# Two graph layers over 64 graphs on one core: the orders of all five engines and the PSUM banks replaced by a new plan

## The reference, cut to what matters

```
# layer 0                                    (adj holds 0 or 1 here)
q, k  = x@Wq+bq, x@Wk+bk
attn  = softmax(q k^T / sqrt(32))            # unmasked, per head
out   = sum_r (attn * (adj==r)) @ (x@Wv[r]+bv[r])
x1    = LN(x + out@Wo + bo) * g1 + beta1
x2    = LN(x1 + gelu(x1@W1+b1)@W2 + b2) * g2 + beta2
# layer 1
e     = leaky_relu(q k^T, 0.2) from x2@Wq, x2@Wk
h     = softmax(where(adj>0, e, -9e15)) @ (x2@Wv)
n1    = LN(h) * g1 + b1
out   = LN(concat(n1, x2) @ Wffn^T) * g2 + b2 + x2
```

## Time and profile before

| | before |
|---|---|
| median of 3 runs | 3199.16 us |
| the runs | 3191.37, 3199.16, 3201.94 us |
| span of the profiled execution | 3190.8 us |
| instructions in the profile | 76499 |
| busy: PE, PEld, DVE, ACT, POOL | 97%, 85%, 82%, 64%, 45% |
| granted TensorE clock, mean | 0.989 |

### The profile page before, as it was taken

One profiled execution on the slowest core, in us unless ns is written; L12 is line 12 of the kernel. 1 busy time (PEld: TensorE's weight loads), 2 busy tenths in 40 slices (PEclk: granted clock), 3 DMA queues, 4 the chain that ended last, 5 costly groups with the idle time before them and its releaser, 6 DMA issues.

```text
span 3190.8 us, 76499 instructions
## 1 busy us (share of the span) xinstructions
PE 3103.2 (97%) x28139; PEld 2715.8 (85%) x28328; DVE 2604.6 (82%) x4896; ACT 2056.7 (64%) x4303; POOL 1432.6 (45%) x1549
## 2 busy tenths in 40 slices
PE   5999999999999999999999999999999999999996
PEld 4888888888888888888888888888888888888885
DVE  4788888888888888888888888888888888888884
ACT  2565766766766766766766766766766766666664
POOL 1445445445445445445445445445344444444441
PEclk8999999999999999999999999999999999999997
DMA  4343344344334334434434434433433433433431
GB/s 111 84 101 93 89 94 97 89 92 98 91 89 98 94 86 98 96 83 98 99 81 98 102 79 97 105 79 94 107 79 92 110 79 89 112 80 89 107 81 31
DMA packets 218074, 292.76 MB, mean 92 GB/s; under 512 B 31796, under 2 KB 119479, under 8 KB 218039
## 3 DMA queue, kind: packets, MB, share of 16 engines
q1 hardware_dynamic: 218038, 292.30, 39.0%
HBM read 73.02 MB, written 16.78 MB: 28 GB/s over the span
## 4 chain that ended last, share of the span: by engine, by line
PE 90%; ACT 3%; issue 3%; DVE 2%; SPq 1%; DMA 1%; POOL 0%; POOLq 0%; DVEq 0%; ACTq 0%
PE pair L994 50%; PE pair L1024 15%; PE pair L1048 7%; PE pair L1038 6%; PE pair L1103 4%; PE pair L1112 2%; PE pair L1040 2%; ACT probs L561 2%; PE pair L1012 2%; SPq L299 1%; PE pair L999 1%; PE pair L1119 0%; ACT leaky_s L540 0%; DMA stack_a<-qk 0%; DMA probs<-in_w 0%
## 5 line engine op out<-in xcount | busy, mean ns | idle before, releaser
L418 POOL TENSOR_TENSOR act_r_lo<-act,act_r_hi 128x512 fp32r<-128x512 f32 x256 | 335.3, 1319 | 741.6 <-DVE act_r_hi L931 537.5
L540 ACT ACTIVATE leaky_s<-leaky_s,low_r 128x256 f32<-128x256 f32 x1024 | 506.1, 499 | 2.7 <-DVE low_r L794 2.0
L424 POOL TENSOR_TENSOR probs<-probs,rel 128x512 f32<-128x512 f32 x256 | 293.4, 1168 | 207.0 <-ACT probs L561 119.8
L561 ACT ACTIVATE probs<-pair 128x1024 f32<-128x1024 f32 x256 | 256.8, 1029 | 189.9 <-PE pair L1112 189.9
L798 DVE TENSOR_REDUCE mx_a<-pair 128x4 f32<-128x1024 f32 x256 | 307.7, 1223 | 78.1 <-PE pair L1103 78.0
L534 ACT ACTIVATE leaky_s<-pair 128x1024 f32<-128x1024 f32 x256 | 262.6, 1026 | 158.7 <-PE pair L1040 158.7
L790 DVE TENSOR_TENSOR leaky_s<-pair,leaky_s 128x1024 f32<-128x1024 f32 x256 | 312.4, 1220 | 37.8 <-ACT leaky_s L534 37.5
L794 DVE TENSOR_REDUCE low_r<-leaky_s 128x4 f32<-128x1024 f32 x256 | 310.8, 1214 | 2.2
L530 ACT ACTIVATE probs<-pair 128x1024 f32<-128x1024 f32 x256 | 261.8, 1023 | 65.1 <-PE pair L1048 60.9
L424 POOL TENSOR_TENSOR leaky_s<-probs,rel 128x512 f32<-128x512 f32 x256 | 291.0, 1173 | 0.2 <-ACT probs L561 0.2
L1048 PE MATMUL pair<-ident,leaky_s 128*128 128x128 f32 x2048 | 269.7, 275 | 6.7 <-ACT leaky_s L540 5.8
(11 more groups left out here) (193 smaller groups left out, 8839.7 us busy)
## 6 DMA issues: line engine op xcount, KB each, us to landing
stack_a<-qk SPq DMA_DIRECT2D x768, 128.0 KB, 2.5
stack_r<-qk SPq DMA_DIRECT2D x768, 128.0 KB, 2.4
xt<-in_xT SPq DMA_DIRECT2D x64, 256.0 KB, 3.4
adj_a<-in_adjT SPq DMA_DIRECT2D x64, 256.0 KB, 3.0
xn<-in_x SPq DMA_DIRECT2D x64, 256.0 KB, 3.2
adj_q<-in_adj SPq DMA_DIRECT2D x64, 256.0 KB, 2.9
out<-n SPq DMA_DIRECT2D x64, 256.0 KB, 2.8
probs<-in_w SPq DMA_DIRECT2D x4, 512.0 KB, 4.6
```

The costliest lines, as they stand in the source:

```text
L418: return nc.gpsimd.tensor_tensor(dst, src, hi, ALU.subtract)
L424: last = nc.gpsimd.tensor_tensor(masked_p[g][:, h], probs[:, g, h], rel1[:], ALU.mult)
L540: last = nc.scalar.activation(leaky_s[:, p % SLOTS, k, t], leaky_s[:, p % SLOTS, k, t], ACT.Exp, bias=low_r[:, p, k, t:t + 1], accum_out=d ...
L561: return nc.scalar.activation(probs[:, g, 2 * q:2 * q + 2], pair[b][:], ACT.Exp, scale=SCALE)
```

## The change

```diff
-        B_AO, B_ADEN, B_Q, B_K, B_WO, B_X1T, B_RV, B_HN = 2, 6, 7, 6, 1, 4, 4, 2
-        B_DN, B_N1T, B_FFN, B_AMT, B_X2T, B_LQ, B_LK, B_LV = 1, 1, 3, 4, 1, 4, 7, 7
+        B_AO, B_ADEN, B_Q, B_K, B_WO, B_X1T, B_RV, B_HN = 3, 2, 2, 4, 1, 5, 7, 5
+        B_N1T, B_DN, B_FFN, B_AMT, B_X2T, B_LQ, B_LK, B_LV = 6, 0, 1, 1, 0, 7, 5, 4
         B_X = 0
-        B_V, B_UP = (5, 7), (4, 6, 1, 5)
-        B_RR, B_TN, B_AR, B_AC = (0, 2, 1, 0), (0, 1, 1, 3), (3, 1, 2, 3), (2, 3, 2, 0)
+        B_V, B_UP = (0, 1), (4, 5, 3, 4)
+        B_RR, B_TN, B_AR, B_AC = (3, 2, 1, 0), (3, 3, 3, 1), (3, 1, 3, 2), (3, 1, 3, 2)
 
         ld_xt, ld_xn, ld_adj_a = sig("ld_xt", 16), sig("ld_xn", 16), sig("ld_adj_a", 16)
...
 def body(g0, g1, g2, g3):
-    if g2 is not None:
-        load(xn, x, g2, "(t p) c -> p t c", ld_xn)
...
+        if ran(g2, 1):
+            sp.wait_ge(off_done.sem, off_done.at(g2 - 1))
+        load(adj_q, adj, g2, "(t p) n -> p t n", ld_adj_r)
     if g1 is not None:
         sp.wait_ge(rqk_split.sem, rqk_split.at(g1))
         stack(0, stack_r, stacked_r)
         stack(1, stack_r, stacked_r)
         stack(2, stack_r, stacked_r)
         stack(3, stack_r, stacked_r)
-    if g2 is not None:
-        load(adj_q, adj, g2, "(t p) n -> p t n", ld_adj_r)
-    if g3 is not None:
+    if g3 is not None:
+        if ran(g3, 1):
+            sp.wait_ge(res_a_done.sem, res_a_done.at(g3 - 1))
+        load(xn, x, g3, "(t p) c -> p t c", ld_xn)
         sp.wait_ge(qk_split.sem, qk_split.at(g3))
         stack(0, stack_a, stacked_a)
         stack(1, stack_a, stacked_a)
         stack(2, stack_a, stacked_a)
         stack(3, stack_a, stacked_a)
-        load(adj_a, adjT, g3, "(t p) n -> p t n", ld_adj_a)
     if g0 is not None:
         sp.wait_ge(ln_done[LN_O].sem, ln_done[LN_O].at(g0))
         sp.dma_start(out[g0 - path.general * G].rearrange("(t p) c -> p t c", p=P), result[:]).then_inc(stored.sem, 16)
+    if g3 is not None:
+        if ran(g3, 1):
+            sp.wait_ge(known_done.sem, known_done.at(g3 - 1))
+        load(adj_a, adjT, g3, "(t p) n -> p t n", ld_adj_a)
...
-    if g0 is not None:
-        pool.wait_ge(ln_mv[LN_H].sem, ln_mv[LN_H].at(g0))
-        make_rstd(LN_H, g0)
-        pool.wait_ge(ln_done[LN_H].sem, ln_done[LN_H].at(g0))
-    if g2 is not None:
...
+        pool.wait_ge(att_hi_done.sem, att_hi_done.at(g2))
+        low(att_lo[:], att[:], att_hi[:]).then_inc(att_split.sem, 1)
...
+    if g3 is not None:
+        dve.wait_ge(qk_hi_done.sem, qk_hi_done.at(g3))
+        biased_low(1, B_K, bk_c).then_inc(qk_split.sem, 1)
+    if g2 is not None:
+        dve.wait_ge(x1t_hi_done.sem, x1t_hi_done.at(g2))
+        lo_part(x1t_lo, B_X1T, x1t_hi).then_inc(x1t_split.sem, 1)
+    if g1 is not None:
+        dve.wait_ge(low_done.sem, low_done.at(g1, 3))
+        leaky(2, B_RR[2]).then_inc(leaky_done.sem, 1)
+    if g2 is not None and not path.general:
+        nc.vector.scalar_tensor_tensor(adj_a[:], adj_a[:], 0, rel1[:], ALU.is_equal, ALU.add,
+                                       accum_out=known[:]).then_inc(known_done.sem, 1)
+    if g1 is not None:
+        dve.wait_ge(leaky_done.sem, leaky_done.at(g1, 3))
+        lowest_row(2).then_inc(low_r_done.sem, 1)
+        dve.wait_ge(low_done.sem, low_done.at(g1))
+        leaky(3, B_RR[3]).then_inc(leaky_done.sem, 1)
     if g2 is not None:
         dve.wait_ge(act_done.sem, act_done.at(g2, 1))
         nc.vector.tensor_copy(act_hi[:, 0], act[:, 0]).then_inc(act_hi_done.sem, 1)
-    if g1 is not None:
-        dve.wait_ge(leaky_done.sem, leaky_done.at(g1))
-        lowest_row(3).then_inc(low_r_done.sem, 1)
-    if g2 is not None:
...
+    if g1 is not None:
+        dve.wait_ge(exp_r_done.sem, exp_r_done.at(g1))
+        nc.vector.reciprocal(rden_r[:], den_r[:]).then_inc(rden_done.sem, 1)
+    if g2 is not None:
+        dve.wait_ge(down_mm.sem, down_mm.at(g2))
+        nc.vector.tensor_tensor(res[:], bank(B_DN), x1[:], ALU.add).then_inc(res_m_done.sem, 1)
+        dve.wait_ge(res_m_done.sem, res_m_done.at(g2))
+        statistics(LN_M, res, g2)
+    if g3 is not None:
+        dve.wait_ge(ld_adj_a.sem, ld_adj_a.at(g3))
+        nc.vector.tensor_scalar(rel1[:], adj_a[:], 1, None, ALU.is_equal).then_inc(rel1_done.sem, 1)
+    if g2 is not None:
+        if ran(g2, 1):
+            dve.wait_ge(x2k_done.sem, x2k_done.at(g2 - 1))
+        dve.wait_ge(ln_mv[LN_M].sem, ln_mv[LN_M].at(g2))
+        centre(LN_M, res, G2, x2)
+        dve.wait_ge(ld_adj_r.sem, ld_adj_r.at(g2))
+        nc.vector.tensor_scalar(off_q[:], adj_q[:], 0, NEG, ALU.is_le, ALU.mult).then_inc(off_done.sem, 1)
+        dve.wait_ge(ln_mid[LN_M].sem, ln_mid[LN_M].at(g2))
+        dve.wait_ge(ln_rstd[LN_M].sem, ln_rstd[LN_M].at(g2))
+        rescale(LN_M, x2, row(E2))
...
         pe.wait_ge(act_split.sem, act_split.at(g2))
         down(3)
     if g1 is not None:
+        pe.wait_ge(probs_r.sem, probs_r.at(g1))
+        row_values(B_RV).then_inc(pvr_mm.sem, 1)
         if ran(g1, -2):
             pe.wait_ge(ashift.sem, ashift.at(g1 + 2))
-        pe.wait_ge(probs_r.sem, probs_r.at(g1))
-        row_values(B_RV).then_inc(pvr_mm.sem, 1)
         half_ffn((x2t_hi, x2t_lo), KT, True).then_inc(ffn_part.sem, 1)
     if g3 is not None:
-        pe.wait_ge(ashifted.sem, ashifted.at(g3))
         if ran(g3, 2):
             pe.wait_ge(att_r_done.sem, att_r_done.at(g3 - 2))
+        pe.wait_ge(ashifted.sem, ashifted.at(g3))
         score_cols(0, B_AC[0]).then_inc(sta_mm.sem, 1)
-        score_cols(1, B_AC[1]).then_inc(sta_mm.sem, 1)
     if g1 is not None:
         pe.wait_ge(att_r_done.sem, att_r_done.at(g1))
         transposed(B_HN, att).then_inc(hn_mm.sem, 1)
+    if g3 is not None:
+        score_cols(1, B_AC[1]).then_inc(sta_mm.sem, 1)
     if g2 is not None:
         pe.wait_ge(ln_done[LN_M].sem, ln_done[LN_M].at(g2))
         transposed(B_X2T, x2).then_inc(x2t_mm.sem, 1)
     if g3 is not None:
         pe.wait_ge(probs_a.sem, probs_a.at(g3, 1))
         score_cols(2, B_AC[2]).then_inc(sta_mm.sem, 1)
-        pe.wait_ge(probs_a.sem, probs_a.at(g3, 2))
         if ran(g3, 2):
             pe.wait_ge(heads_r.sem, heads_r.at(g3 - 2))
+        score_cols(3, B_AC[3]).then_inc(sta_mm.sem, 1)
+        pe.wait_ge(probs_a.sem, probs_a.at(g3, 2))
         both(0).then_inc(pva_mm.sem, 1)
-        if ran(g3, 1):
-            pe.wait_ge(x2t_split.sem, x2t_split.at(g3 - 1))
-        score_cols(3, B_AC[3]).then_inc(sta_mm.sem, 1)
     if g2 is not None:
         if ran(g2, -1):
             pe.wait_ge(probs_a.sem, probs_a.at(g2 + 1, 3))
         pe.wait_ge(x2t_split.sem, x2t_split.at(g2))
         projection("lq", (x2t_hi, x2t_lo), B_LQ).then_inc(rq_mm.sem, 1)
+        if ran(g2, -1):
+            pe.wait_ge(probs_a.sem, probs_a.at(g2 + 1))
         projection("lk", (x2t_hi, x2t_lo), B_LK).then_inc(rq_mm.sem, 1)
     if g1 is not None:
-        if ran(g1, -2):
-            pe.wait_ge(probs_a.sem, probs_a.at(g1 + 2))
         pe.wait_ge(ln_done[LN_H].sem, ln_done[LN_H].at(g1))
         transposed(B_N1T, n1).then_inc(n1t_mm.sem, 1)
     if g3 is not None:
         pe.wait_ge(probs_a.sem, probs_a.at(g3))
         both(1).then_inc(pva_mm.sem, 1)
+        pe.wait_ge(probs1_done.sem, probs1_done.at(g3, 2))
+        one(0).then_inc(pv1_mm.sem, 1)
     if g1 is not None:
         pe.wait_ge(n1t_split.sem, n1t_split.at(g1))
         half_ffn((n1t_hi, n1t_lo), 0, False).then_inc(ffn_mm.sem, 1)
     if g2 is not None:
-        pe.wait_ge(rqk_split.sem, rqk_split.at(g2))
         row_products(B_LV, (x2t_hi, x2t_lo), "lv").then_inc(rv_mm.sem, 1)
         pe.wait_ge(stacked_r[0].sem, stacked_r[0].at(g2))
         masked_rows(0, B_RR[0]).then_inc(sr_mm.sem, 1)
     if g3 is not None:
-        pe.wait_ge(probs1_done.sem, probs1_done.at(g3, 2))
-        one(0).then_inc(pv1_mm.sem, 1)
         pe.wait_ge(probs1_done.sem, probs1_done.at(g3))
         one(1).then_inc(pv1_mm.sem, 1)
         if path.general:
             further_values(g3)
+    if g2 is not None:
+        pe.wait_ge(stacked_r[1].sem, stacked_r[1].at(g2))
+        pe.wait_ge(rv_done.sem, rv_done.at(g2))
+        masked_rows(1, B_RR[1]).then_inc(sr_mm.sem, 1)
```

More of the change, by code:

```diff
@@ L463, in body @@
                 if g0 is not None:
[L464 to L470 removed]
+                    pool.wait_ge(ln_mv[LN_H].sem, ln_mv[LN_H].at(g0))
+                    make_rstd(LN_H, g0)
                 if g2 is not None:
@@ L641, in body @@
                     biased(1, B_K, bk_c).then_inc(qk_hi_done.sem, 1)
+                    copy(v_a[:, 0], bank(B_V[0])).then_inc(v_done.sem, 1)
+                    act_e.wait_ge(v_mm.sem, v_mm.at(g3))
+                    copy(v_a[:, 1], bank(B_V[1])).then_inc(v_done.sem, 1)
                 if g2 is not None:
@@ L848, in body @@
                     lo_part(x2t_lo, B_X2T, x2t_hi).then_inc(x2t_split.sem, 1)
-                    dve.wait_ge(ld_adj_r.sem, ld_adj_r.at(g1))
```

(29 more changed lines are left out.)

210 lines of the change are left out of this document (78 added, 132 removed).

## The result

The changed kernel takes 3180.5 us (median of four, 3179.5 to 3181.0) where the kernel before, run beside it, takes 3197.7: a ratio of 0.9948, 95% interval 0.9934 to 0.9962. It is faster by 17 us. The forecast was 3164, a gain of 35; its range of 3150 to 3197 holds the time, but half of the expected gain did not come.

The account below looks back on a forecast made before the run. TensorE was taken to bound the kernel, its waits being all there was to win: 48.08 - 0.65 + 0.1 = 47.5 us a turn, 0.59 x 60 = 35 us, so 3199.2 - 35.4 = 3164; range 3150 to 3197.

Parts of the forecast that it names:

- The floor of a turn: One loop turn (one graph) on TensorE without waits would take about 47.4 us, against 48.08 before.
- (a): TensorE waits 0.29 us a turn for ScalarE's second exponential ahead of the 32-column products; score_cols(3) moved there fills it.
- (b): Eight score matmuls wait 0.16 us a turn for SyncE's copies into stack_a; starting the copies earlier removes it.
- (c): The last four score matmuls wait 0.07 us a turn for SyncE's copies into stack_a; starting these earlier removes it.
- (d): The first masked_rows group waits 0.09 us a turn for the stack_r copies; one(0) moved ahead of it fills that.
- The thin waits: New near misses where 0.1 to 0.3 us stays in hand; 0.1 us a turn allowed, between 0 and 0.3.
- The cast of chunk 1: VectorE's cast to act_hi held about 1.0 us by GpSimd, lasting near 1.4; costed at nothing, at most 0.67 a turn.
- SP's list, ACT's list: SyncE's reordered loads and their waits, and ScalarE's same instructions with two table loads, were costed at nothing.
- the term for the head norm: VectorE's two rescale passes held by GpSimd's masked products, at most 2 x 0.97 us against 2.2 in hand: no cost.
- rival 1: Only part of the gain: two or three thin waits miss, 0.35 us in all, 0.3 a turn gained; 3181; chance 0.15.
- rival 4: The change doesn't do what it says: VectorE's and GpSimd's passes aren't kept apart; no time or chance given.
- Rivals 2 and 3: No change (second GpSimd hold, or waits misread), 3190 to 3209, chance 0.13; slower (hold at three casts), 3262, 0.10 with others.

Follow-up runs that it names:

- experiment 1: The changed kernel with GpSimd's old order back: masked(0) ahead of n1's rstd, the wait for the finished head norm ahead of masked(1); 3148.8 us.
- experiment 7: The changed kernel in its own order, with masked(0) and masked(1) made in eight GpSimd passes of 256 columns instead of four of 512; 3148.3 us.
- experiment 5: The kernel of experiment 1 with score_cols(3) behind both(0) again on TensorE; 3167.5 us.
- experiment 8: The kernel before, with ScalarE's rounding of k and VectorE's biased_low(1) moved earlier so the copies into stack_a start sooner; 3198.3 us.
- experiment 6: The kernel of experiment 1 with one(0) next to one(1) again, behind masked_rows(0); 3159.7 us.
- experiment 3: The changed kernel with the cast of act chunk 1 moved behind VectorE's first maximum; 3181.4 us.
- experiment 4: The kernel before, with only GpSimd's wait for the end of the head norm ahead of its second masked product removed; 3222.4 us.
- experiment 2: The changed kernel with GpSimd waiting for the end of the head norm ahead of all four masked products; 3173.1 us.

## Why the prediction was right and wrong

- **The floor of a turn, 47.4 us: right.** With every wait gone a turn is 47.44 us (experiments 1 and 7; in experiment 1 constant to 0.01 us from the third turn on). That constancy isn't a property of the kernel before, though: the prediction says that each piece repeats to 0.01 us from turn to turn, but from the sixth mark on the turns of the kernel before lie between 48.01 and 48.15.
- **(a) to (d): right in kind and size.** Forecast 0.29, 0.16, 0.07 and 0.09. The runs give 0.25 for (a) (experiment 5), 0.16 and 0.07 for (b) and (c) (experiment 8, the groups' own durations; together 0.29 on PE's starts) and 0.15 for (d) (experiment 6). These are 0.63 (0.69 with the 0.29) against the 48.08 - 47.44 = 0.64 between the kernel before and experiment 1. All four are gone in the changed kernel.
- **The thin waits, 0.1 us: none came.** The sums with 0.1 to 0.3 in hand held; experiment 1 has no wait but for issue. It is the kernel that the forecast described. Its span is 3145.5 where the forecast's, without the 0.1 (6 us), would be 3149.4; most of the other 3.9 us lies in the first five turns, which had waits of their own before (239.8 us, now 232.2).
- **Two slips in the sum, small beside the miss.** 48.08 - 0.65 + 0.1 is 47.53, which is a gain of 0.55 a turn and not the 0.59 that was used: 33 us and not 35, a forecast of 3166. And the 8.4 us that I added to the span were not a property of the kernel: about 1.8 is what every later run has above its span, the rest is that the profiled execution of the kernel before was a quick one. The median of experiment 1 lies 3.3 above its profiled span.
- **The cast of chunk 1: right.** It was forecast at near 1.4 us and no cost; it is 1.36, and taking it away changes nothing (experiment 3).
- **SP's list, ACT's list: right at nothing.** No wait of PE for a copy is left in the view from 1000 to 2500 us.
- **The step that failed** is the term for the head norm, in the passage on two engines at one port: "By the rows that is at most 2 x 0.97 us, and n1's transposes have 2.2 in hand, so the sum is the same by rule or without." The 2.2 in hand, for which the prediction shows no working, is right (2.1). The hold isn't: I counted two passes and took a hold from line 856 of the opening, 0.97, as the most. There are three, because the rstd now comes ahead of the masked products, so that these begin while the centre's second pass is still to come, and the three together are 2.6 us. Each is 0.87 over its 0.44, less than my 0.97. So it was the count that was wrong, and with a count of three my own row would have given 2.9 against 2.2 and a wait of 0.7. And in the list of GpSimd I wrote only that it no longer waits for ln_done, and priced that removal at nothing. It was the price of the change: experiment 4 takes the same wait out of the kernel before and makes it slower by 26 us; experiment 1 puts the wait and the old order back and wins 32; experiment 7 leaves both as they are, makes the holds short, and wins the same 32.
- **What was luck.** The time lies inside the stated range, but not by the prediction's mechanism. The wait at n1's transposes took 32 us that the forecast had at nothing. That the miss is only 16.5 is because the forecast was too cautious elsewhere: experiment 1, the change without that wait, wins 48 us on medians and not 35.
- **The rivals.** The time is that of rival 1 (3181), again by luck: no thin wait missed by 0.1 or 0.2; one chain with 2.1 in hand missed by 0.5. What happened is nearer to rival 4, which I had dismissed with "the gain of the forecast doesn't rest on that": the change lays the two engines' passes over each other at the one place where that decides the turn. Rivals 2 and 3 put the hold at the casts, where experiment 3 shows that it is free.
- **Not tested:** the 4.8 us that the first five turns gained, and the 1.0 us behind the last mark. I have only their sizes.

## What to carry to other kernels

A wait in a queue may have no data behind it and still have a purpose: here GpSimd waited for VectorE's norm only so that its wide passes would not fall on it. Before such a wait is costed at nothing, list the passes of the other engine that will now run at the same time, one by one, and set the sum of their holds against what is in hand at the step that waits for them. Where the order can't be changed, cutting the wide passes in two did as well here (experiment 7). And when a wait is put back or a step moved ahead, ask who is next in line for what it delays: two of eight experiments removed exactly the wait they were aimed at and gave most of it (experiment 2) or more than all of it (experiment 8) back one step further on.
